# Value products and their evictions at the head of an attention and mixture kernel: two products moved ahead of the second batch's transposes, every fourth eviction given to ScalarE and GpSimd

## What is computed

```python
V = jnp.einsum('bse,hed->bhsd', X, Wv) + bv[None, :, None, :]
A1 = jnp.einsum('bhqd,bhkd->bhqk', Q1, K1) * s
A2 = jnp.einsum('bhqd,bhkd->bhqk', Q2, K2) * s
P = jax.nn.softmax(A1, axis=-1) - lam * jax.nn.softmax(A2, axis=-1)
O = jnp.einsum('bhqk,bhkd->bhqd', P, V)
...
logits = jnp.mean(x, axis=1) @ w_gate + b_gate
probs = jax.nn.softmax(logits, axis=-1)
top_vals, top_idx = lax.top_k(probs, K)
```

## Time and profile before

| What | Value |
|---|---|
| Median of 3 runs | 1177.49 us (1175.26 to 1177.57) |
| Profiled execution, device time | 1176.92 us |
| Its span in the trace | 1175.1 us |
| Granted TensorE clock, mean of full speed | 0.991 |
| PE busy | 1128.0 us, 96% of the span |
| POOL, ACT, DVE busy | 979.9, 949.8 and 904.8 us |
| Value stage and what leads to it | the first 46.6 us |

### The profile page before, as it was taken

One profiled execution on the slowest core, in us unless ns is written; L12 is line 12 of the kernel. 1 busy time (PEld: TensorE's weight loads), 2 busy tenths in 40 slices (PEclk: granted clock), 3 DMA queues, 4 the chain that ended last, 5 costly groups with the idle time before them and its releaser, 6 DMA issues.

```text
span 1175.1 us, 27816 instructions
## 1 busy us (share of the span) xinstructions
PE 1128.0 (96%) x9730; PEld 779.9 (66%) x9730; DVE 904.8 (77%) x1573; ACT 949.8 (81%) x1711; POOL 979.9 (83%) x609
## 2 busy tenths in 40 slices
PE   5899999999999999999999999999999999998998
PEld 4666666666666666666666666666666666664797
DVE  7878888888888888888888888888888888874510
ACT  3288899888898888898888898888898988885432
POOL 2589999999999999998888999999898888899000
PEclk9999999999999999999999999999999999998999
DMA  8942222222211222122212211222222212100000
GB/s 196 344 115 61 48 63 61 61 61 62 53 42 44 61 61 56 45 78 56 55 46 56 50 35 37 56 56 56 56 56 56 56 45 56 43 5 1 1 19 18
DMA packets 76439, 71.28 MB, mean 61 GB/s; under 512 B 43380, under 2 KB 65396, under 8 KB 76404
## 3 DMA queue, kind: packets, MB, share of 16 engines
q1 hardware_dynamic: 75396, 70.65, 23.1%
q10 hardware_dynamic: 880, 0.19, 0.1%
q0 software_dynamic: 128, 0.01, 0.0%
HBM read 22.59 MB, written 14.68 MB: 32 GB/s over the span
## 4 chain that ended last, share of the span: by engine, by line
PE 63%; ACT 20%; issue 6%; POOL 6%; DVE 4%; ACTq 1%; DMA 0%; DVEq 0%; SPq 0%; POOLq 0%
PE ps L567 20%; PE ps L535 18%; ACT work L753 11%; PE ps L553 10%; PE ps L489 8%; ACT p_mix L753 6%; POOL p_mix L448 3%; PE ps L652 3%; ACT pt L766 3%; PE ps L639 2%; POOL work L445 2%; PE ps L516 1%; DVE small L947 1%; DVE pt L903 1%; ACT small L719 0%
## 5 line engine op out<-in xcount | busy, mean ns | idle before, releaser
L947 DVE TENSOR_REDUCE small<-ps 128x1 f32<-128x1024 f32 x512 | 614.3, 1220 | 168.3 <-PE ps L535 168.3
L448 POOL TENSOR_TENSOR p_mix<-p_mix,work 128x1024 f32<-128x1024 f32 x256 | 608.8, 2378 | 21.4
L766 ACT ACTIVATE pt<-ps 128x512 f32<-128x512 f32 x512 | 306.8, 599 | 131.8 <-PE ps L553 129.7
L553 PE MATMUL ps<-ident,p_mix 64*128 64x64 f32 x4096 | 353.1, 227 | 5.6 <-POOL p_mix L448 2.8
L445 POOL TENSOR_SCALAR work<-work,small 128x1024 f32<-128x1024 f32 x256 | 307.4, 1201 | 50.4 <-DVE small L972 48.3
L553 PEld LDWEIGHTS ps<-ident,p_mix 64*128 64x128 f32 x4096 | 305.6, 139 | 55.9 <-issue 37.2
L753 ACT ACTIVATE p_mix<-ps,small 128x1024 f32<-128x1024 f32 x256 | 286.5, 1119 | 16.7 <-DVE small L947 16.7
L753 ACT ACTIVATE work<-ps,small 128x1024 f32<-128x1024 f32 x256 | 285.1, 1114 | 0.1
L567 PE MATMUL ps<-pt,v_h 128*64 128x512 f32 x1024 | 250.2, 610 | 0.7 <-ACT pt L766 0.7
L535 PE MATMUL ps<-k_hi,q_hi 64*128 64x512 f32 x512 | 227.5, 444 | 5.9 <-ACT p_mix L753 3.4
L535 PE MATMUL ps<-k_hi,q_lo 64*128 64x512 f32 x512 | 225.8, 441 | 0.0
(11 more groups left out here) (135 smaller groups left out, 1211.0 us busy)
## 6 DMA issues: line engine op xcount, KB each, us to landing
qx_hi<-q_hi SPq DMA_DIRECT2D x64, 256.0 KB, 3.8
qx_lo<-q_lo SPq DMA_DIRECT2D x64, 256.0 KB, 4.6
v_scratch<-pt SPq DMA_DIRECT2D x16, 512.0 KB, 5.4
v_h<-v_scratch SPq DMA_DIRECT2D x32, 256.0 KB, 3.1
w_scratch<-wqk_hi SPq DMA_DIRECT2D x16, 160.0 KB, 1.8
w_scratch<-wqk_lo SPq DMA_DIRECT2D x16, 160.0 KB, 1.9
wqk_hi<-w_scratch SPq DMA_DIRECT2D x16, 160.0 KB, 2.2
wqk_lo<-w_scratch SPq DMA_DIRECT2D x16, 160.0 KB, 2.3
```

Of the source, the lines that this page charges most:

```text
L448: pool.tensor_tensor(e1, e1, e2, ALU.add).then_inc(mix_done, 1)
L553: mm = pe.transpose(pt_ps[:, c * D:(c + 1) * D], p_mix[rows, col:col + P], ident[rows, rows])
L766: act.activation(pt4[:, kb % 2, :, j * P + half * D:j * P + (half + 1) * D], pt_ps.rearrange("p (c q) -> p c q", c=KC), ACT.Copy).then_inc ...
L947: dve.tensor_reduce(neg_max[:, m:m + 1], slot[SLOT[k, s]], AX.X, ALU.max, negate=True)\
```

## The change

Three things are different. First, PE computes value parts 0 and 1 ahead of `turn_x(1)` instead of behind it. Second, parts 3, 7, ... 31 are evicted by ACT as a plain copy (`copy_v`, counted by `v_copied`), and POOL then adds the bias in SBUF (`bias_v`, counted by `v_added`); DVE evicts the other 24, and a store waits for both counts. Third, on POOL `start_y` stands behind the split of head 1's weights and waits for the normalised tokens; behind it stand six bias additions, then `set_main`, then the last two additions.

```diff
             for i in range(NT):
-                sp.wait_ge(v_evac, 2 * i + 2)
+                sp.wait_ge(v_evac, 2 * i + 2 - (i + 1) // 2)
+                after(sp, v_added, (i + 1) // 2)
                 sp.dma_start(v_scratch[i, :, :], v_st[:, i % TB, :]).then_inc(v_stored[i % TB], 16)
...
-            start_y()
             for n in range(1, NW):
                 split_w(n)
+            pool.wait_ge(xn_ready, 2 * B)
+            start_y()
+
+            def bias_v(first, end):
+
+                for u in range(first, end, 4):
+                    pool.wait_ge(v_copied, u // 4 + 1)
+                    hv = u % 2
+                    pool.tensor_tensor(v_part(u), v_part(u), bv_bc[:, hv * BANK:(hv + 1) * BANK], ALU.add)\
+                        .then_inc(v_added, 1)
+
+            bias_v(3, 24)
             set_main()
+            bias_v(27, 2 * NT)
...
+            pe.wait_ge(wv_split, 2)
+            values(0)
+            values(1)
             turn_x(1)
...
+            for u in range(2, 2 * NT):
...
+                values(u)
+
+
+            pe.wait_ge(v_copied, 2 * NT // 4)
+            pe.wait_ge(v_evac, 2 * NT - 2 * NT // 4)
...
+            def copy_v(u):
+
+                act.wait_ge(v_mm, u + 1)
+                after(act, v_stored[u // 2 % TB], 16 * (u // 2 // TB))
+                act.activation(v_part(u), v_bank(u), ACT.Copy).then_inc(v_copied, 1)
+
+            for u in range(3, 16, 4):
+                copy_v(u)
             act.wait_ge(route, 5)
             act.activation(prob, logit, ACT.Exp, bias=lg_max, scale=1.0, accum_out=lg_sum).then_inc(route_act, 1)
+            for u in range(19, 2 * NT, 4):
+                copy_v(u)
...
                 for u in range(first, end):
                     i, hv = divmod(u, 2)
-                    bank = 4 + (u + 2) % 4
+                    if by_act(u):
+                        continue
                     dve.wait_ge(v_mm, u + 1)
```

More of the change, by code:

```diff
@@ L144, in build @@
         wv_split, v_mm, v_evac = sem("wv_split"), sem("v_mm"), sem("v_evac")
+        v_copied, v_added = sem("v_copied"), sem("v_added")
         v_stored = [sem(f"v_stored{i}") for i in range(TB)]
@@ L203, in slot_free, with by_act, v_part, v_bank @@
             return exp_done, 2 * (g * BODY + k) + what + 1
+        def by_act(u):
+            return u % 4 == 3
+        def v_part(u):
+            i, hv = divmod(u, 2)
+            return v_st[:, i % TB, hv * BANK:(hv + 1) * BANK]
+        def v_bank(u):
+            bank = 4 + (u + 2) % 4
+            return ps[:, bank * BANK:(bank + 1) * BANK]
         def xt_bank(i):
@@ L496, in _ @@
             proj(0, 0, 32, 1, slot[2])
-            turn_x(1)
[L500 to L503, removed]
-                    bank = 4 + (u + 2) % 4
[L505 to L518, removed]
@@ L521, in _, with values @@
-            pe.wait_ge(v_evac, 2 * NT)
+            def values(u):
+                i, hv = divmod(u, 2)
+                if u == 2:
+                    pe.wait_ge(lo_done, 2)
+                if u % 8 == 0:
+                    pe.wait_ge(xt_lo, i // 4 + 1)
+                if by_act(u):
+                    after(pe, v_copied, u // 4)
+                else:
+                    after(pe, v_evac, u - 3 - (u - 3) // 4)
+                for j, (a, w) in enumerate(((xT_hi, wv_hi), (xT_lo, wv_hi), (xT_hi, wv_lo))):
+                    mm = pe.matmul(v_bank(u), a[:, i * P:(i + 1) * P],
+                                   w[:, hv * BANK:(hv + 1) * BANK], start=j == 0, stop=j == 2)
+                mm.then_inc(v_mm, 1)
@@ new lines, in _ @@
+            pe.wait_ge(wv_split, 2)
+            values(0)
+            values(1)
+            turn_x(1)
+            for u in range(2, 2 * NT):
+                if u == 14:
+                    pe.wait_ge(route, 2)
+                    pe.wait_ge(small_loaded, 64)
+                    pe.matmul(ps[0:B, 2 * BANK:2 * BANK + NEXP], mean_tok, wg, start=True, stop=True)\
+                        .then_inc(route_mm, 1)
+                values(u)
+            pe.wait_ge(v_copied, 2 * NT // 4)
+            pe.wait_ge(v_evac, 2 * NT - 2 * NT // 4)
@@ L902, in evac_v @@
                         after(dve, v_stored[i % TB], 16 * (i // TB))
-                    dve.tensor_tensor(v_st[:, i % TB, hv * BANK:(hv + 1) * BANK],
-                                      ps[:, bank * BANK:(bank + 1) * BANK],
-                                      bv_bc[:, hv * BANK:(hv + 1) * BANK], ALU.add).then_inc(v_evac, 1)
+                    dve.tensor_tensor(v_part(u), v_bank(u), bv_bc[:, hv * BANK:(hv + 1) * BANK], ALU.add)\
+                        .then_inc(v_evac, 1)
             low_part(0, 0, 0, slot[0])
```

## The result

The changed kernel runs in 1179.95 us (median of 16 runs, 1177.8 to 1184.81), the kernel before beside it in 1177.53 us. The ratio is 1.0024, with a 95% interval from 1.0013 to 1.0035: slower, by 2.8 us on 1177.5 (the two medians lie 2.4 us apart). One of the 16 runs of the kernel before took 1624.59 us, for a reason that no trace shows; without it the median of before is 1177.49. The profiled execution took 1178.75 us with a span of 1176.9 us, where the one before had 1176.92 and 1175.1.

What follows compares the result with a forecast made beforehand. Before the first scores PE, not DVE, was taken to set the pace, with little slack in the stores. Terms -1.13 and +6.2 made +5.1 us on 1176.92, 1182.0, taken as 1182.3; overall range 1178.6 to 1185.

Steps and rivals of the forecast that it cites:

- The fill: DVE's tiny instruction, held by GpSimd's accumulator fill, falls from 1.32 to 0.19 us; part 4 starts 1.13 us earlier.
- The two products: Six early matmuls on PE before the transposes gain nothing: part 4 still waits for DVE's first eviction.
- The share: DVE losing 8 of 32 evictions saves only pauses, since PE sets the pace; a GpSimd addition takes 1.19 us.
- The wait that decides: Store 1 waits for GpSimd's first addition, issued at 33.7 instead of 27.7; late staging tiles hold up parts 18 onward.
- The slow clock: PE idles 3.0 us before part 28, then runs three of parts 28 to 31 at 1.2 GHz, 1.28 us each.
- rival with the clock up: Same store wait but PE's clock stays up: +3.6 us, 1180.8 us, chance 0.25.
- The term of the sum for the stage: The value stage before the scores: +6.2 us for the store wait and the slow clock.
- Go through to the end: Attention steps follow each other by data, so the scores' 5.1 us delay reaches the end in full.
- my likeliest case: Whole kernel with store wait and slow clock: 1182.3 us, own range 1181 to 1184, chance 0.50.

Runs made afterwards that it cites:

- the late store alone: Kernel before with the fill moved, DVE evicting all 32 parts, stores from the second on waiting for GpSimd's fill: 1179.82 us, ratio 1.0034, scores at 48.67.
- the additions taken away: Changed kernel without GpSimd's eight bias additions, stores waiting for ScalarE's copies instead: 1175.21 us, ratio 0.9996 against the kernel before, scores at 45.30.
- the share only: Changed kernel with the fill in GpSimd's idle stretch, part 3's addition ahead of the split, both products behind the transposes: 1175.73 us, ratio 1.0001.
- the fill alone in the gap: Kernel before with only GpSimd's fill moved into its idle stretch, as soon as the tokens are normalised: 1174.64 us, ratio 0.9987, scores at 45.06.

## Why the prediction was right, and where it was off

**The fill.** Right: 1.32 became 0.17 us, and the evictions start 1.33 us earlier (1.13 forecast; DVE's rows stood 0.1 to 0.2 us earlier already ahead of this instruction). That it is GpSimd's fill that held the instruction is shown by the two kernels that moved it alone and by the one that moved it back. The rule of the Trainium skill, page "SBUF — State Buffer", section "Who interferes with whom", held again on a small routing instruction with two inputs beside an addition: 1.27 us in four kernels, against 0.13 without an addition beside it. A routing instruction with one input beside its scalar, L970 of the changed kernel, took 1.29 us beside the fifth addition, against 0.22 elsewhere, which the sentence on two inputs doesn't cover. I had not counted these; in the changed kernel this pause ended before the landing of store 2 and cost nothing.

**The two products.** Right for the total ("they gain nothing"), but the working left out the clock: PE's idle time behind the transposes brought parts 2 and 3 into a slow stretch, and part 4 started at 24.82 instead of 24.37. Where the stores do not bind, they cost 1.2 us in one pair of kernels and 0.9 in another, and the kernel without the additions, which has them early too, shows no such cost (45.30).

**The share.** Right: by itself it saves nothing (45.24 against 45.14, one trace each). The addition costs 1.27 us (1.19 forecast).

**The wait that decides.** Right in its mechanism and nearly in its numbers: store 1 at 33.4 (33.7 forecast), store 2 at 36.7 (37.1), store 4 at 42.3 (41.8; stores 2 and 3 took 1.89 us to issue instead of 0.90). The size that was off is the landing of store 4, 2.8 us instead of 4.0, as the profile shows when asked for this store alone:

```profile
DMA to landing us min/median/max: 2.8/2.8/2.8
```

So part 24 was evicted from 45.17 (45.8 forecast), and stores 5 to 7 came 0.5 to 0.6 us earlier too. The last wait of the stage is that of part 31 for store 7. It was issued at 44.0, and its row is

```profile
DMA to landing us min/median/max: 5.0/5.0/5.0
```

It landed at 49.0 (49.5 forecast), ScalarE copied part 31 from 49.10, and the scores followed. PE's last value product ended at 48.96, so at the end the store and PE came out within 0.1 us of each other. Store 15 was issued 5.7 us later than before (4.4 forecast), more than the 3.3 us of the scores; the first three attention steps, late by no more than 3.3 us, show no wait for it. Shown by the late store alone and by the additions taken away.

**The slow clock.** The step that failed. I put it on parts 28 to 31, behind an idle stretch of 3.0 us at 43.4 to 46.4, and charged 1.5 us for it. PE did idle for 2.52 us and the clock did fall, but one wait earlier, between parts 23 and 24; PE ran at 1.2 GHz from 42.1 to about 45.4, through most of parts 24 to 27, and this filled the time in which it would have waited for store 4 anyway. Parts 28 to 31 ran at full speed, and the scores started at 49.90, behind a last eviction that ended at 49.70, near the 50.1 of my rival with the clock up: its number came out, though not its reason. The term of the sum for the stage was +6.2 and measured +4.6 (49.90 against the 45.30 of the kernel without additions).

**"Go through to the end".** Half right. GpSimd's first attention step was late by 3.28 us (55.68 against 52.40) and the second and third as much; the fourth only by 2.2. The rows of the fourth, in the changed kernel and in the kernel before:

```profile
68.10 1.20 POOL L472 TENSOR_SCALAR work<-work,small 128x1024 f32<-128x1024 f32 x1 [0.95 <-DVE small L1015]
```

```profile
65.93 1.19 POOL L445 TENSOR_SCALAR work<-work,small 128x1024 f32<-128x1024 f32 x1 [2.07 <-DVE small L972]
```

In between, the kernel before had its slow stretch (60.8 to 64.2) and the changed one did not. Whether that belongs to the change is open. None of the four kernels with a late first store has a slow stretch between 59 and 65, and six of the eight others have one (the last two to be run do not), with one trace of each. So part of what the late store costs may be won back there, against what I had said. Later the lag of the changed kernel is 2.5 us (at 1001.70 in the kernel before) and 2.6 at the last scaling (1084.24 against 1081.66). Over 16 runs the difference is 2.8 us by the ratio, between the 3.3 of the scores and the 1.8 of the two spans. I had forecast 1182.3, and the median is 1179.95. It lies in the overall range, but below that of my likeliest case (1181 to 1184) and nearest to the rival with the clock up (1180.8): that the range holds it is owed to the rivals that it was widened for, not to the working of the likeliest case.

## What to carry to other kernels

When work moves to an idle engine, look at what its program has in front of that work, and at who waits for the result: here eight additions of 1.27 us cost next to nothing by themselves, and the place of the first of them behind a load, a split and a fill held back a queue of stores and the buffers that they release. The engine that waits most is not the one to relieve if another sets the pace; a pace read from one row (0.72 us a part on PE, 0.61 on DVE) told that before any run. And the side edit may be the one worth keeping: the fill alone, out of DVE's way, took the scores from 46.6 to 45.1 and left the additions unneeded, though its gain in the total (1.5 us by both ratios) is still inside the intervals.

## What the runs showed of the hardware

The scatter of the totals goes in the main with the clock. In the first set of 35 runs of the kernel before, the median was 1175.4 us for the nine with a mean granted clock of 0.994, 1176.4 for the twelve with 0.991, and 1181.3 for the three with 0.986; but the three with 0.993 took 1178.8, so the mean clock alone doesn't give the time. In the first 100 us the slow stretches move with small edits. One stands behind an idle time of PE of 2.52 us in the changed kernel (39.1 to 41.6), one behind 1.85 us in the kernel with the fill and the products moved (20.2 to 22.1), and in the kernels with the share only and with the fill alone in the gap there is none between 20 and 100. Behind the first scores PE idled for 1.41 and 0.87 us with the fill moved and for 1.41 and 0.96 us in the kernel before; in the first the clock fell at 50.8, ahead of the second of these idle times, and rose at 57.6; in the second kernel it stayed up there. What decides between these two was not tested.
